# Cross attention with its context rows padded to 3072 bytes, its operands at one remainder of 512, and its shared context tails loaded two chunks at a time

## The chip, the cores and the metric

The kernel runs on one core of a Trainium2 chip. The metric is the device time of one launch in microseconds (us); lower is better.

## The reference

A decoder layer on x (32 examples of 100 tokens, 512 wide) with a context of 32 x 722 x 512, everything in float32. A layer norm without learned scale follows each of its three parts. Cut to what matters:

```python
x = layernorm(x + self_attention(x))                 # 16 heads of 32, with a distance factor
x = layernorm(x + cross_attention(x, context))       # the part that changes
x = layernorm(x + ffn(x))                            # 512 -> 1536 (gate, up) -> 512

def cross_attention(x, c):                           # per example: x 100 x 512, c 722 x 512
    q, k, v = x @ Wq.T + bq, c @ Wk.T + bk, c @ Wv.T + bv
    scores = q * 32**-0.5 @ k.T                      # per head, 100 x 722
    return softmax(scores) @ v @ Wo.T + bo
```

## The kernel before

Three stages follow each other. Tiles whose names begin with A_ and C_ belong to self attention and its output and query projections, D_ to cross attention, E_ to the output projection of cross attention and the feed-forward part. Each float32 operand of a projection is split into a high part (rounded to the matmul's format) and a low part (the rest), and a product takes three matmuls: high x high, high x low and low x high. With 512 inputs in four chunks of 128, `products` (L68) issues 12 matmuls into one bank of PSUM. Each matmul has a weight load of its own (a stationary operand of 128 columns, 512 bytes in each partition), which the profile shows as PEld beside the matmul before it.

**Cross attention** runs over 32 examples b, 8 steps for each. For each example TensorE makes 8 *key units* (4 groups of four heads, called quads, times two halves of the context: stationary a slice of `cross_wk`, moving 362 or 360 columns of the context, `HALVES`) and up to 6 *value units* (stationary 128 rows of the context, moving 512 columns of `cross_wv`). For each quad it makes the scores (`scores`, in even steps) and, six steps after a quad's first step, the weighted sum (`weighted_sum`, 48 matmuls). All units take turns in two banks, `D_ps_p`; a unit waits (`wait_bank`) until the bank that was filled two units before has been read. So that reading is ordered, too: ScalarE reads the values of a step (`take_values`) behind `normalise_second` of that step, which waits for the reciprocal that VectorE makes behind its transposes.

Between scores and weighted sum lie: VectorE's maxima, ScalarE's exponentials, the reciprocal, the normalising (GpSimd the first head of a step, ScalarE the second), VectorE's transposes of 32 x 32 blocks into `D_turned` (`turn_blocks`), and 16 DMAs for each quad that move the blocks to other partitions, `D_turned` to `D_pT`: 12 from SP's queue (`move`, L1361), 4 from ScalarE's. `D_turned` has two buffers, so `turn_blocks` of quad n waits until the moves of quad n - 2 have landed.

**SP's queue** is strictly in program order. For each b: the queries of b + 1 (`load_q`), the moves of quad 4b - 1, two chunks of the context of b + 2 (`load_ctx`), the moves of quad 4b, the store of b - 1, the moves of 4b + 1, two more chunks of the context, the moves of 4b + 2.

**Tails.** 722 context rows are five tiles of 128 and a rest of 82. To save value units, the rests of four examples share three tiles of 128 rows (examples 4q + 2 to 4q + 5, for q = 0 to 6). `load_tails(q)` loads them raw into `D_tails_raw`, all four chunks, with six DMAs, in iteration b = 4q - 1 (for q = 0 before the loop). GpSimd splits them chunk by chunk (`split_tails`, high L1496, low L1499), at the steps 8(4q + 1) + (-2, 1, 2, 3, 6, 6, 9, 9) of `TAIL_STEP`: high of chunk 0, low of chunk 0, high of chunk 1, and so on. Only then are the raw tiles free.

**Places in SBUF.** Each tile begins at a multiple of 32 bytes. The weights `cross_wk`, `cross_wv` (8192 bytes for each part) and `D_ctx0` (even examples) begin at one remainder of 512, that of `nc.sbuf_base`. A chunk of the context takes 722 x 4 = 2888 bytes = 5 x 512 + 328, a part 11552 = 22 x 512 + 288, and both parts of an example `one_ctx` = 23104 = 45 x 512 + 64. So the chunks of the two examples' buffers lie at many remainders. `E_wo` begins at `raw_at`, the activations `E_acts` at `even_at` = `nc.sbuf_base`; between the two lie 2 x 23104 = 90 x 512 + 128 bytes. The hidden tiles of the feed-forward part (30720 = 60 x 512 bytes each, token tiles of 512 bytes) and its weight pieces 5 to 11 (6144 = 12 x 512) both begin a multiple of 512 from `rest_at`.

Of the kernel before, what the change touches and what calls it, by code (L numbers as in the profile page):

```python
# [8 lines left out]
B, T, S, D, H = 32, 100, 722, 512, 16  # L9
HD = D // H  # L10
# [113 lines left out]
def phase_self_attention(nc, sem, passed, xT, wq, wk, wv, w, v, v_d, rows_d, o_d, x, bo, bq, x1_d, cq_d, raws, cross_w,  # L124
# [25 lines left out]
    with ExitStack() as ctx, ExitStack() as of_attention, ExitStack() as of_units, ExitStack() as of_outputs:  # L150
# [117 lines left out]
        for s in range(B):  # L268
# [25 lines left out]
        ctx0 = Split(lambda n, shape, dt: nc.alloc_sbuf_tensor_at(n, shape, dt, offset=ctx_at + (n[-3:] == "low") * 4 * KD * S),  # L294
                     "D_ctx0", [P, KD, S])
# [21 lines left out]
        with nc.Block() as block:  # L317
# [182 lines left out]
            def _(pool):  # L500
# [79 lines left out]
                for g in range(NG):  # L580
                    for i in range(TT):
                        n = TT * g + i
                        pool.wait_ge(eps_done, n + 1)
                        wait(pool, x1_done, n - 1)
                        pool.tensor_tensor(rstd[n % 2][:, :], var_eps[n % 2][:, :], minus_half[:, :], ALU.pow)\
                            .then_inc(rstd_done, 1)
                        if i + 2 < TT:
                            add_bias(g, i + 2)
                        elif g < 2:
                            add_bias(g + 1, i + 2 - TT)  # L590
                    if 2 <= g < NG - 1:
                        add_bias(g + 1, 0)
                        add_bias(g + 1, 1)
                    if 1 <= g < NG - 1:
                        for i in range(TT):
                            low_o(g + 1, i)
                    if 1 <= g < 3:
                        c_low(pool, [g + 1])
                for k in range(KD):
                    pool.wait_ge(ctx0_high, k + 1)  # L600
                    pool.tensor_tensor(ctx0[1][:, k, :], ctx0_raw[k], ctx0[0][:, k, :].bitcast(F32), ALU.subtract)\
                        .then_inc(ctx0_low, 1)
# [3 lines left out]
            def _(act):  # L606
# [116 lines left out]
                for k in range(KD):  # L723
                    act.activation(ctx0[0][:, k, :], ctx0_raw[k], ACT.Copy).then_inc(ctx0_high, 1)
# [311 lines left out]
def phase_cross_and_feed_forward(nc, sem, passed, ctxT, cq_d, held, bk, bv, o_d, x1_d, wo, bo, w_gate, w_up, w_down, biggest, out):  # L1036
# [20 lines left out]
    HALVES = ((0, 362), (362, S))  # L1057
# [25 lines left out]
    with ExitStack() as ctx:  # L1083
        W, ident, minus_half, biggest1, biggest_all, inexact, ctx0, q_stored = held
        every_weight = 2 * 2 * KD * D * 4
        one_ctx = 2 * KD * S * 4
# [51 lines left out]
        first_x1 = [*x1b, None, None, middle("E_x1_last", [P, D])]  # L1138
        r = {"a": middle("E_r_a", [P, D])}
        y = [middle(f"E_y{i}", [P, D]) for i in range(2)]  # L1140
        first_x1[2:4] = y
        stats = {n: even("E_stats_" + n, [P, 6]) for n in "ab"}
        mv = {n: even("E_mv_" + n, [P, 2]) for n in "ab"}
        var_eps = {n: even("E_var_eps_" + n, [P, 1]) for n in "ab"}
        rstd = {n: even("E_rstd_" + n, [P, 1]) for n in "ab"}
# [5 lines left out]
        x2 = first("E_x2", [P, TT, D])  # L1151
        r["b"] = odd("E_r_b", [P, D])
# [29 lines left out]
        t_loaded, t_high, t_low = sem("D_t_loaded"), sem("D_t_high"), sem("D_t_low")  # L1182
# [93 lines left out]
        x1_loaded, x1b_done = [sem("E_x1_loaded0"), sem("E_x1_loaded1")], sem("E_x1b_done")  # L1276
        y_done, t_done, th_done, tl_done = (sem("E_" + n) for n in ("y_done", "t_done", "th_done", "tl_done"))
# [39 lines left out]
        def x1_rows(g, i):  # L1317

            return (x1b[i % 2] if later(g) else first_x1[i])[:, :]
# [5 lines left out]
        with nc.Block() as block:  # L1325

            @block.sync
            def _(sp):
# [8 lines left out]
                def load_tails(q):  # L1337
                    wait(sp, t_low, KD * q)
                    for i in range(3):
                        sp.dma_start(tails_raw[:, :, i * P:i * P + LAST], c_rows[4 * q + 2 + i, :, :, FULL:S])\  # L1340
                          .then_inc(t_loaded, 16)
                    for i in range(3):
                        first, end = FULL + THIRD * i, min(FULL + THIRD * (i + 1), S)
                        sp.dma_start(tails_raw[:, :, (i + 1) * P - THIRD:(i + 1) * P - THIRD + end - first],
                                     c_rows[4 * q + 5, :, :, first:end]).then_inc(t_loaded, 16)
# [86 lines left out]
                for i in range(TT):  # L1432
                    sp.dma_start(first_x1[i][:, :], x1_d[col(i * P, P), :]).then_inc(x1_loaded[i % 2], 16)
# [3 lines left out]
                sp.wait_ge(u_done, len(unit_count))  # L1437
                load_weights(0)
# [30 lines left out]
            def _(pool):  # L1469
# [12 lines left out]
                def split_piece(b, k):  # L1482
                    if k == 0:
                        wait(pool, u_done, max((unit_count[i] for i in unit_count if i[1] == b - 2), default=0))
                    wait_apart(pool, c_loaded[k % 2], 32 * (b - 1) + 16 * (k // 2) + 16, passed)
                    pool.tensor_copy(cs[b % 2][0][:, k, :], craw[k % 2][:, :]).then_inc(c_high, 1)
                    pool.wait_ge(c_high, KD * b + k + 1)
                    pool.tensor_tensor(cs[b % 2][1][:, k, :], craw[k % 2][:, :],  # L1488
                                       cs[b % 2][0][:, k, :].bitcast(F32), ALU.subtract).then_inc(c_low, 1)

                def split_tails(q, k, low):
                    if k == 0 and not low:
                        wait(pool, u_done, unit_count["v", 4 * q, ST - 1] if q else 0)
                        pool.wait_ge(t_loaded, 96 * (q + 1))
                    if not low:
                        pool.tensor_copy(tails[0][:, k, :], tails_raw[:, k, :]).then_inc(t_high, 1)  # L1496
                    else:
                        pool.wait_ge(t_high, KD * q + k + 1)
                        pool.tensor_tensor(tails[1][:, k, :], tails_raw[:, k, :], tails[0][:, k, :].bitcast(F32),  # L1499
# [4 lines left out]
                def add_bias(g, i):  # L1504
                    if later(g):
                        pool.wait_ge(x1_loaded[i % 2], 16 * slot_count(g, i) + 16)
                    else:
                        pool.wait_ge(x1_loaded[i % 2], 16 * slot_count(1, i % 2))
# [631 lines left out]
```

## Time and profile before

| | |
|---|---|
| median of 3 runs | 2404.95 us (2403.91 to 2406.62) |
| profiled execution: its own time | 2403.91 us |
| profiled execution: span in the trace | 2402.1 us, mean granted TensorE clock 0.992 |
| TensorE busy | 2351.1 us of the span (98%) |
| VectorE, GpSimd, ScalarE busy | 1510.7, 1384.9, 1330.2 us |

The span goes from the first to the last instruction. Matmuls are pipelined and their ends are modelled, so the time that one takes from the stream is the distance between the starts of two neighbours, not its busy time. A granted clock of 1.00 is 2.4 GHz, 0.50 is 1.2 GHz. SP is not among the busy engines: its rows give the time that it spends issuing DMAs.

### The profile page before, as it was taken

The page shows a single profiled execution, that of the slowest core. Times are in us where ns is not written, and L with a number is a line of the kernel's source. Part 1 is how long each engine was busy: PE and PEld are TensorE (multiplying, and loading weights), DVE is VectorE, ACT ScalarE, POOL GpSimd, SP SyncE. Part 2 cuts the span into 40 slices and gives each one's busy share as a digit, 9 for nine tenths or more (in the row PEclk, how much of TensorE's full clock was granted, in tenths as well). Part 3 has the DMA queues.
Part 4 walks back from the last instruction along what each step waited for, and adds up shares of the span by engine and source line. Part 5 has one row for each costly group of instructions (what it writes and reads, how often), then busy time and mean ns, then how long its engine had stood idle before and what let it go on. Part 6 is the DMA issues. An engine that isn't in the chain of part 4 may idle for free.

```text
span 2402.1 us, 58639 instructions
## 1 busy us (share of the span) xinstructions
PE 2351.1 (98%) x21642; PEld 2041.4 (85%) x21642; DVE 1510.7 (63%) x2562; ACT 1330.2 (55%) x3322; POOL 1384.9 (58%) x1212
## 2 busy tenths in 40 slices
PE   8999989999999999999999999999999899999999
PEld 7888758988888888888888888888888699998998
DVE  4666688836767677676767677676766734435342
ACT  5888852236666666666666666666666541221321
POOL 4777577447667567566666667667664533333332
PEclk9999989999999999999999999999999999999999
DMA  7444468537677777777776776777677831102010
GB/s 193 133 127 123 119 192 323 203 105 198 185 194 200 192 199 190 193 203 197 183 206 190 201 195 190 197 196 196 186 193 201 240 124 43 49 17 65 5 35 23
DMA packets 254121, 384.59 MB, mean 160 GB/s; under 512 B 116056, under 2 KB 131480, under 8 KB 253848
## 3 DMA queue, kind: packets, MB, share of 16 engines
q1 hardware_dynamic: 229272, 330.65, 48.5%
q10 hardware_dynamic: 24576, 50.36, 8.3%
q8 instruction: 164, 2.69, 0.5%
q14 instruction: 109, 0.89, 0.1%
HBM read 126.33 MB, written 40.60 MB: 69 GB/s over the span
## 4 chain that ended last, share of the span: by engine, by line
PE 75%; DVE 1%; issue 1%; SPq 1%; DMA 1%; POOL 1%; ACT 0%; ACTq 0%; DVEq 0%; POOLq 0%
PE D_ps_p L68 42%; PE D_ps_s L1941 7%; PE D_ps_p L1968 6%; PE E_ps_g L68 6%; PE E_ps_u L68 6%; PE E_ps_d L68 5%; PE E_ps_y L68 3%; SPq L1361 1%; DVE D_columns L1745 0%; PE E_ps_t L1994 0%; ACT D_e L1610 0%; DVE D_turned L1759 0%; DMA D_pT<-D_turned 0%; DMA E_w_int<-in_w_gate 0%; POOL E_acts_low L1533 0%
## 5 line engine op out<-in xcount | busy, mean ns | idle before, releaser
L1473 POOL TENSOR_SCALAR D_e<-D_e,D_columns 128x722 f32<-128x722 f32 x256 | 538.5, 2104 | 468.2 <-DVE D_columns L1751 468.1
L1610 ACT ACTIVATE D_e<-D_ps_s,D_columns 128x723 f32<-128x723 f32 x512 | 437.7, 861 | 392.5 <-DVE D_columns L1745 347.6
L1745 DVE TENSOR_REDUCE D_columns<-D_ps_s 128x1 f32<-128x723 f32 x512 | 439.6, 900 | 296.6 <-PE D_ps_s L1941 296.5
L1759 DVE STREAM_TRANSPOSE D_turned<-D_e 128x768 f32<-128x768 f32 x512 | 496.2, 973 | 14.0 <-DMA D_pT<-D_turned 13.2
L68 PE MATMUL D_ps_p<-D_ctx_high,cross_wk_high 128*128 128x362 f32 (+1 forms) x1024 | 350.1, 342 | 1.9 <-DVEq L1771 1.5
L68 PE MATMUL D_ps_p<-D_ctx_low,cross_wk_high 128*128 128x362 f32 (+1 forms) x1024 | 336.7, 329 | 0.0
L68 PE MATMUL D_ps_p<-D_ctx_high,cross_wk_low 128*128 128x362 f32 (+1 forms) x1024 | 334.9, 327 | 0.0
L68 PE MATMUL D_ps_p<-cross_wv_high,D_ctx_high 128*128 128x512 f32 (+1 forms) x656 | 259.7, 396 | 0.0
L68 PE MATMUL D_ps_p<-cross_wv_high,D_ctx_low 128*128 128x512 f32 (+1 forms) x656 | 259.3, 395 | 0.0
L68 PE MATMUL D_ps_p<-cross_wv_low,D_ctx_high 128*128 128x512 f32 (+1 forms) x656 | 257.7, 393 | 0.0
L1617 ACT ACTIVATE D_e<-D_e,D_columns 128x722 f32<-128x722 f32 x256 | 231.0, 902 | 8.9 <-DVE D_columns L1751 8.9
L68 PEld LDWEIGHTS D_ps_p<-D_ctx_high,cross_wk_high 128*128 128x128 f32 x1024 | 192.5, 188 | 24.5 <-issue 19.4
L1528 POOL TENSOR_TENSOR E_hidden_low<-E_gated,E_hidden_high 128x320 fp32r<-128x320 f32 x120 | 104.9, 876 | 186.0 <-ACT E_hidden_high L1675 186.0
L1488 POOL TENSOR_TENSOR D_ctx_low<-D_craw,D_ctx_high 128x722 fp32r<-128x722 f32 x124 | 198.7, 1603 | 17.7 <-issue 7.1
L646 ACT ACTIVATE A_e<-A_e,A_neg_max 100x100 f32<-100x100 f32 x512 | 186.1, 367 | 40.9 <-DVE A_neg_max L773 40.6
L68 PEld LDWEIGHTS D_ps_p<-D_ctx_low,cross_wk_high 128*128 128x128 f32 x1024 | 193.2, 189 | 2.4
L1941 PE MATMUL D_ps_s<-D_keys,D_queries 32*128 32x241 f32 (+1 forms) x3072 | 192.5, 378 | 2.6 <-ACT D_e L1610 2.6
L68 PEld LDWEIGHTS D_ps_p<-D_ctx_high,cross_wk_low 128*128 128x128 f32 x1024 | 193.0, 188 | 0.0
L1852 DVE SCALAR_TENSOR_TENSOR E_gated<-E_ps_u,E_gated 128x320 f32<-128x320 f32 x120 | 59.0, 492 | 212.5 <-ACT E_gated L1682 212.5
L1941 PEld LDWEIGHTS D_ps_s<-D_keys,D_queries 32*128 32x128 f32 x3072 | 134.1, 184 | 59.9 <-issue 49.5
L1599 ACT ACTIVATE D_values<-D_ps_p 128x512 f32<-128x512 f32 (+1 forms) x185 | 110.0, 595 | 96.1 <-PE D_ps_p L68 96.0
L1968 PEld LDWEIGHTS D_ps_p<-D_pT,D_values 128*32 128x32 f32 x5920 | 126.0, 108 | 39.6 <-issue 38.9
(257 smaller groups left out, 5248.5 us busy)
## 6 DMA issues: line engine op xcount, KB each, us to landing
D_pT<-D_turned SPq DMA_DIRECT2D x1536, 96.0 KB, 2.5
D_pT<-D_turned ACTq DMA_DIRECT2D x512, 96.0 KB, 2.7
D_craw<-in_ctxT SPq DMA_DIRECT2D x124, 361.0 KB, 4.0
self_v<-wstage SPq DMA_DIRECT2D x25, 256.0 KB, 2.5
A_v<-self_v SPq DMA_DIRECT2D x32, 200.0 KB
self_o<-A_o SPq DMA_DIRECT2D x32, 200.0 KB, 3.6
x<-C_x SPq DMA_DIRECT2D x5, 1280.0 KB, 5.2
cross_q<-C_qo SPq DMA_DIRECT2D x20, 320.0 KB, 4.0
```

Source lines behind the costliest of these rows:

```text
L68: last = pe.matmul(out, lhs(a, k), rhs(b, k), start=(k == 0 and n == 0), stop=(k == chunks - 1 and n == len(terms) - 1))
L646: act.activation(head, head, ACT.Exp, bias=neg_max[:, b % 2, h:h + 1], accum_out=rowsum[:, half, i:i + 1]).then_inc(exp_done, 1)
L1473: pool.tensor_scalar(head, head, inv[:, 2 * (s % 2):2 * (s % 2) + 1], None, ALU.mult)\
L1488: pool.tensor_tensor(cs[b % 2][1][:, k, :], craw[k % 2][:, :], cs[b % 2][0][:, k, :].bitcast(F32), ALU.subtract).then_inc(c_low, 1)
L1528: pool.tensor_tensor(hs[1][:, c, cols], gated[u % 2][:, :], hs[0][:, c, cols].bitcast(F32), ALU.subtract).then_inc(hl_done, 1)
L1599: act.activation(vs[b % 2][0:rows, i, :], bank("v", b, i)[0:rows, 0:D], ACT.Copy).then_inc(v_done, 1)
L1610: act.activation(e[n // 2 % 2][:, n % 2, 0:PARTS * PART].rearrange("p (a c) -> p a c", a=PARTS), parts_of(n), ACT.Exp, bias=neg_max[:, n % ...
L1617: act.activation(head, head, ACT.Copy, scale=inv[:, 2 * (s % 2) + 1:2 * (s % 2) + 2])\
L1745: dve.tensor_reduce(neg_max[:, n % 4:n % 4 + 1], parts_of(n), AX.XY, ALU.max, negate=True)\
L1759: dve.transpose(turned[quad % 2][:, :, 2 * (s % 2) + h, :].rearrange("p j (t r) -> p t j r", r=32), e[s % 2][:, h, :].rearrange("p (t j r) ...
L1941: return pe.matmul(of_head[:, j, a, 0:end - first], qs[rows, m, :, :].rearrange("p a q -> p (a q)"), ks[rows, m, first:end], start=True, s ...
L1968: last = pe.matmul(out[HD * j:HD * (j + 1), 0:T], values[:, c:c + HD], pT[quad % 2][:, :, j, 32 * i:32 * i + QB], start=(i == 0), stop=(i ...
```

## The change

- A context chunk is spaced 768 x 4 = 3072 bytes (`ROW`) in `D_ctx0` and `D_ctx1`; only its first 722 columns are written and read. The halves of the keys become 384 and 338 columns. `one_ctx` becomes 24576 = 48 x 512.
- `D_tails` and `D_values_fourth` are placed right behind `D_ctx1`, so that all of them, the weights and the context chunks begin at one remainder of 512. `E_wo` begins there too, since `raw_at - even_at` is now 96 x 512.
- The room comes from `D_tails_raw`: two chunks in place of four. `load_tails(q, k)` loads one chunk with six DMAs and waits until the low part of the chunk that had its half before is done (`t_low` at 4q + k - 1). Chunks 0 and 1 are loaded where all four were loaded before; chunk 2 at the end of iteration b = 4q, behind the moves of quad 16q + 2; chunk 3 in iteration b = 4q + 1, behind the moves of quad 16q + 4.
- Small tiles of the E stage change places; the last tile of `x1` is loaded later, into `E_x2`, behind the last unit. GpSimd's split of the first context waits for `biggest_done`, since its place now reaches a tile that is read for it.

```diff
+ROW = 768
...
+                pool.wait_ge(biggest_done, 3 * KD)
                 for k in range(KD):
                     pool.wait_ge(ctx0_high, k + 1)
...
-    HALVES = ((0, 362), (362, S))
+    HALVES = ((0, ROW // 2), (ROW // 2, S))
...
-        one_ctx = 2 * KD * S * 4
+        one_ctx = 2 * KD * ROW * 4
...
-        cs = [ctx0, Split(inputs, "D_ctx1", [P, KD, S])]
+        cs = [ctx0, Split(inputs, "D_ctx1", [P, KD, ROW])]
         raw_at = inputs.at
-        craw = [inputs(f"D_craw{i}", [P, S]) for i in range(2)]
-
-        tails_raw = inputs("D_tails_raw", [P, KD, 3 * P])
         tails = Split(inputs, "D_tails", [P, KD, 3 * P])
         fourth = [inputs(f"D_values_fourth{i}", [P, D]) for i in range(2)]
+        craw = [inputs(f"D_craw{i}", [P, S]) for i in range(2)]
+        tails_raw = inputs("D_tails_raw", [P, 2, 3 * P])
...
-                def load_tails(q):
-                    wait(sp, t_low, KD * q)
+                def load_tails(q, k):
+                    n = KD * q + k
+                    wait(sp, t_low, n - 1)
                     for i in range(3):
-                        sp.dma_start(tails_raw[:, :, i * P:i * P + LAST], c_rows[4 * q + 2 + i, :, :, FULL:S])\
-                          .then_inc(t_loaded, 16)
+                        sp.dma_start(tails_raw[:, k % 2, i * P:i * P + LAST], c_rows[4 * q + 2 + i, :, k, FULL:S])\
+                          .then_inc(t_loaded[k % 2], 16)
...
-                load_tails(0)
+                load_tails(0, 0)
+                load_tails(0, 1)
                 for b in range(B - 1):
                     load_q(b + 1)
...
                     move(QUADS * b)
+                    if b % 4 == 1 and b // 4 < FOURS:
+                        load_tails(b // 4, 3)
                     if b > 0:
                         store(b - 1)
...
                     if b % 4 == 3 and (b + 1) // 4 < FOURS:
-                        load_tails((b + 1) // 4)
+                        load_tails((b + 1) // 4, 0)
+                        load_tails((b + 1) // 4, 1)
                     move(QUADS * b + 1)
...
                     move(QUADS * b + 2)
+                    if b % 4 == 0 and b // 4 < FOURS:
+                        load_tails(b // 4, 2)
...
+                load_first_x1(TT - 1)
                 load_weights(0)
...
                     if not low:
-                        pool.tensor_copy(tails[0][:, k, :], tails_raw[:, k, :]).then_inc(t_high, 1)
+                        pool.wait_ge(t_loaded[k % 2], 96 * (2 * q + k // 2 + 1))
+                        pool.tensor_copy(tails[0][:, k, :], tails_raw[:, k % 2, :]).then_inc(t_high, 1)
```

## Rows read from the trace of the kernel before

**Rows 1.** The page: span, and busy us with share of each engine.
```profile
span 2402.1 us, 58639 instructions
PE 2351.1 (98%) x21642; PEld 2041.4 (85%) x21642; DVE 1510.7 (63%) x2562; ACT 1330.2 (55%) x3322; POOL 1384.9 (58%) x1212
```

**Rows 2.** Busy us by stretch: cross attention's steady part; PEclk is the clock.
```profile
520.00:1860.00 1340.00, 1339.45 (x13957) 1141.74 (x13956) 927.23 (x1612) 866.00 (x1691) 870.98 (x671) 1.00 0.72 194
```

**Rows 3.** Timeline of PE: first and last of 12 matmuls, key unit, value unit.
```profile
1200.42 0.33 PE L68 MATMUL D_ps_p<-D_ctx_high,cross_wk_high 128*128 128x360 f32 x1
...
1202.25 0.32 PE L68 MATMUL D_ps_p<-D_ctx_high,cross_wk_low 128*128 128x360 f32 x1
1202.41 0.39 PE L68 MATMUL D_ps_p<-cross_wv_high,D_ctx_high 128*128 128x512 f32 x1
...
1204.97 0.39 PE L68 MATMUL D_ps_p<-cross_wv_high,D_ctx_low 128*128 128x512 f32 x1
```

**Rows 4.** Timeline of PE, E stage: within 24 E_ps_d matmuls, then 12 E_ps_y.
```profile
2004.15 0.39 PE L68 MATMUL E_ps_d<-E_w_f32r,E_hidden_low 128*128 128x512 f32 x1
...
2006.67 0.39 PE L68 MATMUL E_ps_d<-E_w_f32r,E_hidden_high 128*128 128x512 f32 x1
...
2009.16 0.40 PE L68 MATMUL E_ps_d<-E_w_f32r,E_hidden_low 128*128 128x512 f32 x1
2009.39 0.40 PE L68 MATMUL E_ps_y<-E_wo_high,E_acts_high 128*128 128x512 f32 x1
...
2011.95 0.40 PE L68 MATMUL E_ps_y<-E_wo_high,E_acts_low 128*128 128x512 f32 x1
```

**Rows 5.** Groups of PE by shape: count | busy us, mean ns | idle before.
```profile
L68 PE MATMUL D_ps_p<-cross_wv_high,D_ctx_high 128*128 128x512 f32 x640 | 253.4, 396 | 0.0
...
L68 PE MATMUL D_ps_p<-D_ctx_low,cross_wk_high 128*128 128x362 f32 x512 | 169.0, 330 | 0.0
...
L68 PE MATMUL D_ps_p<-cross_wv_high,D_tails_high 128*128 128x512 f32 x84 | 33.1, 395 | 0.0
```

**Rows 6.** Timeline of GpSimd and SP's queue near 740 us: start, length.
```profile
724.03 8.73 SPq L1361 DMA_DIRECT2D D_pT<-D_turned  x12
732.81 0.59 SPq L1349 DMA_DIRECT2D D_qraw<-cross_q  x1
733.50 7.54 SPq L1361 DMA_DIRECT2D D_pT<-D_turned  x12
...
740.32 0.99 POOL L1499 TENSOR_TENSOR D_tails_low<-D_tails_raw,D_tails_high 128x384 fp32r<-128x384 f32 x1
```

**Rows 7.** Timeline of SP's queue: the six loads of four tail chunks.
```profile
1014.52 1.65 SPq L1340 DMA_DIRECT2D D_tails_raw<-in_ctxT  x3
1016.22 1.87 SPq L1344 DMA_DIRECT2D D_tails_raw<-in_ctxT  x3
```

**Rows 8.** The moves in the stretch from 520 us: time from issue to landing.
```profile
DMA to landing us min/median/max: 2.0/2.6/9.5
```

**Rows 9.** Timeline of PE: weighted sum of quad 19 and the key unit behind.
```profile
751.33 1.24 PE L1968 MATMUL D_ps_p<-D_pT,D_values 128*32 128x100 f32 x48
752.49 0.43 PE L68 MATMUL D_ps_p<-D_ctx_high,cross_wk_high 128*128 128x362 f32 x1
```

**Rows 10.** Timelines of VectorE and ScalarE: a first transpose of quad 21, values.
```profile
747.28 0.97 DVE L1759 STREAM_TRANSPOSE D_turned<-D_e 128x768 f32<-128x768 f32 x1
...
750.33 0.59 ACT L1599 ACTIVATE D_values<-D_ps_p 128x512 f32<-128x512 f32 x1
```

**Rows 11.** Busy us by stretch at the end of cross attention, columns as in 2.
```profile
1870.00:1877.50 7.50, 3.86 (x77) 2.59 (x75) 5.95 (x12) 5.41 (x11) 7.50 (x6) 1.00 1.03 288
1877.50:1881.00 3.50, 3.47 (x8) 2.79 (x9) 2.44 (x4) 2.45 (x6) 3.50 (x3) 0.51 1.09 284
```

**Rows 12.** VectorE's maxima of the integer weights; GpSimd's first work in cross attention.
```profile
L844 DVE TENSOR_TENSOR biggest<-biggest,C_piece_max x9: 159/627/1076, 406.6 to 479.1; 128x1 f32<-128x1 f32 x9
...
492.22 1.38 POOL L1543 MEMSET D_tails_raw<- 128x1536 f32 x1 [8.92 <-POOLq L317]
```

More of the change, by code:

```diff
@@ L293, in phase_self_attention @@
         ctx_at = nc.sbuf_base
-        ctx0 = Split(lambda n, shape, dt: nc.alloc_sbuf_tensor_at(n, shape, dt, offset=ctx_at + (n[-3:] == "low") * 4 * KD * S),
-                     "D_ctx0", [P, KD, S])
+        ctx0 = Split(lambda n, shape, dt: nc.alloc_sbuf_tensor_at(n, shape, dt, offset=ctx_at + (n[-3:] == "low") * 4 * KD * ROW),
+                     "D_ctx0", [P, KD, ROW])
         ctx0_raw = [staging[k // 2][:, :, :].rearrange("p k n -> p (k n)")[:, k % 2 * S:(k % 2 + 1) * S] for k in range(KD)]
@@ L723, in _ @@
                 for k in range(KD):
-                    act.activation(ctx0[0][:, k, :], ctx0_raw[k], ACT.Copy).then_inc(ctx0_high, 1)
+                    act.activation(ctx0[0][:, k, 0:S], ctx0_raw[k], ACT.Copy).then_inc(ctx0_high, 1)
                 act.wait_ge(ctx0_high, KD)
@@ L1137, in phase_cross_and_feed_forward @@
         x1b = [middle(f"E_x1b{i}", [P, D]) for i in range(2)]
-        first_x1 = [*x1b, None, None, middle("E_x1_last", [P, D])]
-        r = {"a": middle("E_r_a", [P, D])}
+        r = {"a": even("E_r_a", [P, D])}
         y = [middle(f"E_y{i}", [P, D]) for i in range(2)]
[L1141 to L1145, printed above, removed]
+        stats = {n: middle("E_stats_" + n, [P, 6]) for n in "ab"}
+        mv = {n: middle("E_mv_" + n, [P, 2]) for n in "ab"}
+        var_eps = {n: middle("E_var_eps_" + n, [P, 1]) for n in "ab"}
+        rstd = {n: middle("E_rstd_" + n, [P, 1]) for n in "ab"}
         EARLY = 5
@@ L1151, in phase_cross_and_feed_forward @@
         x2 = first("E_x2", [P, TT, D])
+        first_x1 = [t[:, :] for t in (*x1b, *y)] + [x2[:, TT - 1, :]]
         r["b"] = odd("E_r_b", [P, D])
@@ L1317, in x1_rows @@
         def x1_rows(g, i):
-            return (x1b[i % 2] if later(g) else first_x1[i])[:, :]
+            return x1b[i % 2][:, :] if later(g) else first_x1[i]
         def place(t, n):
@@ L1335, in load_ctx @@
                     sp.dma_start(craw[k % 2][:, :], c_rows[b, :, k, :]).then_inc(c_loaded[k % 2], 16)
[L1337 to L1338 removed]
+                def load_tails(q, k):
+                    n = KD * q + k
+                    wait(sp, t_low, n - 1)
                     for i in range(3):
[L1340 to L1341 removed]
+                        sp.dma_start(tails_raw[:, k % 2, i * P:i * P + LAST], c_rows[4 * q + 2 + i, :, k, FULL:S])\
+                          .then_inc(t_loaded[k % 2], 16)
                     for i in range(3):
                         first, end = FULL + THIRD * i, min(FULL + THIRD * (i + 1), S)
[L1344 to L1345 removed]
+                        sp.dma_start(tails_raw[:, k % 2, (i + 1) * P - THIRD:(i + 1) * P - THIRD + end - first],
+                                     c_rows[4 * q + 5, :, k, first:end]).then_inc(t_loaded[k % 2], 16)
                 def load_q(b):
@@ L1431, in _, with load_first_x1 @@
                 sp.dma_start(bo_b[:, :], bo.rearrange("(a n) -> a n", a=1).broadcast_to([P, D])).then_inc(bo_loaded, 16)
-                for i in range(TT):
-                    sp.dma_start(first_x1[i][:, :], x1_d[col(i * P, P), :]).then_inc(x1_loaded[i % 2], 16)
+                def load_first_x1(i):
+                    sp.dma_start(first_x1[i], x1_d[col(i * P, P), :])\
+                      .then_inc(x1_loaded[i % 2] if i < TT - 1 else x1_last_loaded, 16)
+                for i in range(TT - 1):
+                    load_first_x1(i)
                 move(last - 3)
```

20 lines of the change are left out of this document (11 added, 9 removed).

## The prediction

> **What bounds the kernel now.** I read the page first: TensorE is busy 98% of the span, the others at most 63% [rows 1]. Then the busy time by stretch: in cross attention's steady part, 1340 us and more than half of the span, TensorE is busy 1339.45 us at the full clock [rows 2]. So there a nanosecond saved for each matmul is saved from the time, and every us for which TensorE has to wait is added to it. Next the timeline of TensorE, for the distance between starts. A value unit's 12 matmuls start from 1202.41 to 1204.97 us, 2.56/11 = 232.7 ns apart, a key unit's 360-column ones 1.83/11 = 166.4 ns apart [rows 3]. At 2.4 GHz 512 and 360 columns are 213.3 and 150.0 ns, so 19.4 and 16.4 ns come on top of the columns.
>
> Last SP's queue, since the change adds DMAs and waits there. The 12 moves of a quad take it 7.54 to 8.73 us, and those of the next begin 9.47 us after those of the last (724.03, 733.50) [rows 6]. It is in order and has little room. The reader is to see the lead that it has: the last of the moves of quad 19 is issued at 733.50 + 7.54 = 741.04 and lands about 2 us later, and the weighted sum of this quad starts at 751.33 [rows 6, 8, 9]: some 8 us.
>
> **Alignment, the gain.** The trace has 512-column matmuls whose two operands begin at one remainder of 512 (E_ps_d) beside others that lie 128 bytes apart (E_ps_y), at one clock. E_ps_y: 2.56/11 = 232.7 ns, as the value units. E_ps_d: (2009.16 - 2006.67)/11 = 226.4 ns once the run is settled, (2006.67 - 2004.15)/11 = 229.1 ns in the eleven before [rows 4]. So one remainder is worth 3.6 ns early in a run and 6.3 ns late. A value unit is 12 long, but its neighbours will be aligned too: I take 5.0. There are 3 x (640 + 84) = 2172 such matmuls [rows 5]: 10.9 us (7.8 to 13.7). The key matmuls, 6 x 512 = 3072 [rows 5] (the 360-column groups have the same count), have 16.4 ns over their columns, and the aligned run 13.0 at the best, 15.8 early: 0.6 to 3.4 ns, middle 2.0: 6.1 us (1.8 to 10.4). 384 + 338 columns are as many as 362 + 360. `E_wo` gets the activations' remainder: 300 matmuls by 5.0 ns, 1.5 us. Together **-18.5 us** (-10.7 to -26).
>
> There is a rule against this term. The Trainium skill, "TensorE: Matmul & The Clock Gate", Part 2, step-by-step, says that TensorE reads the moving operand and the next weights through two independent ports, so that loading weights takes nothing from the running matmul. By it the remainders of the two could not matter and this term would be 0; the two runs in [rows 4], of one shape and clock, speak against it.
>
> **The tail loads, the price.** Chunk 2 of the tails goes where chunk 0 lay, so SP may load it only after the low part of chunk 0. It is placed behind the moves of quad 16q + 2. For q = 1: these moves are issued by 724.03 + 8.73 = 732.76; the low part of chunk 0 ends at 740.32 + 0.99 = 741.31 [rows 6]. SP stands for 8.5 us, and behind it stand `load_q` and the moves of quad 19, which before began at 733.50. Step by step:
>
> - 741.31: SP goes on. Six loads take 3.57 us before [rows 7]; the new ones move a quarter of the bytes each, but issue costs by the instruction, as far as these rows go (`load_q` costs 0.59): 3.5 (1.8 to 3.6). 744.8.
> - `load_q` 0.7: 745.5. The 12 moves 7.54 to 8.73 [rows 6], I take 8.1: 753.6.
> - The last one lands 2.6 us after its issue began (2.0 at the least) [rows 8], 2.0 after it ended: 755.6.
> - The weighted sum of quad 19, at 751.33 before [rows 9], waits 4.3 us.
> - What is late next: the transposes of quad 21 use the buffer that these moves read. The first stood at 747.28 and would now be at 755.6, 8.3 us late. Behind it in order stand the reciprocals, ScalarE's normalising and the values read out at 750.33 to 750.92: 3.64 us after that transpose began [rows 10]. So 759.2. The key unit behind the weighted sum fills the bank that these values leave; it began at 752.49 [rows 9]. TensorE loses 759.2 - 752.49 = 6.7 us in all.
>
> This comes for each q from 0 to 6, as the program repeats by four examples: 7 x 6.7 = **+47 us**. Bounds: with loads at half the issue time, moves at 7.54 and landing 1.4 us behind, the transpose is at 752.7 and the loss 3.9: 27 us. With 3.6, 8.73 and 2.0 it is at 756.3 and the loss 7.5: 52 us. Nothing earlier gives it back: TensorE has no idle time to fill.
>
> **Chunks 0 and 1** are 12 loads where six stood: 3.5 us later for the moves behind, six times (q = 1 to 6). Without delay a weighted sum has 8 us in hand; six loads take 3.6 of them now, 3.5 more leave 1. The transposes behind have 752.49 - 750.92 = 1.57 us [rows 9, 10]. I take 0.5 for each: **+3 us** (0 to 12). Chunk 3 waits for work that is long done by then, and its 3.5 us fall where SP is already late and TensorE too: 0.
>
> **The clock.** After 7.5 us in which TensorE was busy for 3.86, the next 3.5 us had a granted clock of 0.51, the level of 1.2 GHz [rows 11]. The new wait, 4.3 us and 2.4 us around one weighted sum, leaves TensorE as idle. 3.4 us at half clock lose 1.7 us, of which part falls into the second wait: 0 to 1.7 each, I take 0.9, **+6 us** (0 to 12).
>
> **At nothing.** GpSimd's split of the first context may now begin only after the last maximum, at about 479.7; it ended at 492.22 - 8.92 = 483.3 and then waited 8.92 us for the stage to begin [rows 12]. A delay of 3 us or so is covered by that; without it, 3 us once. The smaller memset behind it saves under a us that nothing waits for. The copies into padded rows, and ScalarE's 384 or 338 columns in place of 362 and 360, are as many elements on engines with a third of their time free [rows 2]. The late load of the last `x1` tile costs SP one issue, 0.6 us, at the end.
>
> **Sum**, against the profiled execution's own 2403.9 us (1 us below the median shown): 2403.9 + 47 + 3 + 6 - 18.5 = **2441 us**.
>
> **Rivals and chances.**
>
> 1. As above, both mechanisms: 2441 us. 0.60.
> 2. *Alignment brings nothing*, because the difference in [rows 4] comes from something else in these runs (their length, the neighbours): 2403.9 + 47 + 3 + 6 = 2460 us. For it: the spacings of units differ little; against it: two values in one stage at one clock. 0.15. The Trainium skill's rule on two independent ports, weighed above, would bring this.
> 3. *Only half of the stall*: the weighted sum waits 4.3 us, but the chain behind it is absorbed (ScalarE's order has slack that I don't see) and the clock holds: 7 x 4.3 = 30; 2403.9 + 30 - 18.5 = 2415 us. For it: engines beside TensorE are idle a third of the time; against it: bank and order force the chain. 0.15.
> 4. *The stall is hidden, and it is faster*: the wait costs only SP's lead. It decides at the transpose: it may start 1.57 us late, at 748.85, so SP would have to go on by about 734.5 rather than 741.3. That needs the low part of chunk 0 some 7 us earlier against the moves. Then 2403.9 - 18.5 = 2385 us. For it: SP has leads of 8 us elsewhere; against it: GpSimd's place for this operation isn't moved. 0.08.
>
> 0.02 is left for more (a longer half clock). To break even, the loss would have to be 18.5/7 = 2.6 us at each of the seven places; the lower bound is 3.9.
>
> **Range.** Low: 27 us of stall, no clock, 26 us of gain: 2405. High: 52 + 12 + 6 - 11: 2463. I give 2407 to 2464, which holds the first two cases and most of the third. The three runs lie 2.7 us apart, so 0.2%, 4.8 us, is about what a measurement tells from no change. Faster: case 4, 0.08. Within 0.2%: the lower part of case 3, 0.05. Slower: 0.87.
>
> **What the profile of the changed kernel would show.** Seven places, one for every four examples, where the weighted sum of quad 16q + 3 waits for the moves (some 4 us), and the key unit behind it for ScalarE's values (some 2.4 us); in SP's queue a gap of 8 us before the loads of chunk 2, released by GpSimd's low part of chunk 0; VectorE's transposes waiting for moves far longer than before. Value matmuls 227 to 229 ns apart, 384-column keys 173 to 175 (160.0 + 13 to 15), E_ps_y 227 to 229. Half-clock stretches behind some of the seven. It would be wrong if SP were not kept waiting there, if the weighted sum found its moves landed, or if the distances stayed at 233 ns.

## The result, and the profile after

The changed kernel takes 2454.9 us (median of 6 runs, 2451.93 to 2455.83) where the one before took 2404.55 in runs beside it: 1.0207 times as long, 95% interval 1.0197 to 1.0217. That is slower by 50 us; the forecast was 2441 with a range of 2407 to 2464. All medians in this document are of fast runs; the only slow ones are two of the eleven of the kernel with late loads on the layout of before (2567 and 4147 us).

The profiled execution took 2455.3 us. The page of the changed kernel, busy time and share of each engine as in [rows 1]:

```profile
span 2453.5 us, 58766 instructions
PE 2360.7 (96%) x21642; PEld 2055.6 (84%) x21642; DVE 1509.0 (62%) x2562; ACT 1335.4 (54%) x3322; POOL 1402.4 (57%) x1212
```

The span is 51.4 us longer, and TensorE's busy time only 9.6 us. So TensorE waits, or works slowly, or both. What it waits for in the steady part of cross attention (520 to 1900 us; total us, times, longest us):

```profile
PE D_ps_p L1983 <- DMA D_pT<-D_turned: 25.5, 7, 4.2
PE D_ps_p L69 <- ACT D_values L1614: 12.0, 11, 2.2
```

L1983 is the weighted sum (L1968 before), L69 the helper of the projections (L68 before), L1614 the values read out. Seven weighted sums wait for their moves, and the units behind them for ScalarE. Together 37.5 us; in [rows 2] TensorE was idle for half a microsecond. The changed kernel's waits of SP's queue and of VectorE (the latter from 520 to 1900 us) show what lies ahead of that:

```profile
SPq L1342 <- POOL D_tails_low L1512: 65.0, 7, 11.4
...
DVE D_turned L1774 <- DMA D_pT<-D_turned: 135.9, 44, 9.2
```

One of the seven places, step by step: the changed kernel's timelines around 760 us, GpSimd, SP's queue, TensorE, VectorE, ScalarE, in this order (start, length; in brackets the idle time before and what ended it):

```profile
747.33 1.00 POOL L1512 TENSOR_TENSOR D_tails_low<-D_tails_raw,D_tails_high 128x384 fp32r<-128x384 f32 x1
...
748.36 2.58 SPq L1342 DMA_DIRECT2D D_tails_raw<-in_ctxT  x3
750.98 1.39 SPq L1346 DMA_DIRECT2D D_tails_raw<-in_ctxT  x3
752.41 0.43 SPq L1351 DMA_DIRECT2D D_qraw<-cross_q  x1
752.94 7.59 SPq L1363 DMA_DIRECT2D D_pT<-D_turned  x12
...
762.17 1.25 PE L1983 MATMUL D_ps_p<-D_pT,D_values 128*32 128x100 f32 x48 [3.98 <-DMA D_pT<-D_turned]
765.63 0.69 PE L69 MATMUL D_ps_p<-D_ctx_high,cross_wk_high 128*128 128x384 f32 x1 [2.21 <-ACT D_values L1614]
766.12 0.52 PE L69 MATMUL D_ps_p<-D_ctx_low,cross_wk_high 128*128 128x384 f32 x1
766.44 0.52 PE L69 MATMUL D_ps_p<-D_ctx_high,cross_wk_low 128*128 128x384 f32 x1
...
762.22 0.98 DVE L1774 STREAM_TRANSPOSE D_turned<-D_e 128x768 f32<-128x768 f32 x1 [7.97 <-DMA D_pT<-D_turned]
...
764.20 0.90 ACT L1632 ACTIVATE D_e<-D_e,D_columns 128x722 f32<-128x722 f32 x1 [7.68 <-DVE D_columns L1766]
765.00 0.58 ACT L1614 ACTIVATE D_values<-D_ps_p 128x512 f32<-128x512 f32 x1
```

GpSimd ends the low part at 748.33; SP goes on at 748.36, issues six loads, the queries' load and twelve moves until 760.53; the moves have landed at 762.17, when the weighted sum starts 3.98 us late. In the same moment VectorE starts its transposes, 7.97 us late; ScalarE's normalising and values follow, and the key unit behind the weighted sum has waited 2.21 us more. That is the prediction's chain, with 13.84 us from the end of the low part to the weighted sum where 14.3 (741.31 to 755.6) were forecast, 3.46 to the key unit (3.6 forecast), and 6.19 us of idle TensorE (6.7 forecast).

The last two TensorE rows start 0.32 us apart for 384 columns. That is the lower clock. The changed kernel's windows at the seven places (TensorE busy, then the granted clock):

```profile
582.48:589.28 6.80, 5.34 (x56) 0.50 0.76 230
763.38:770.18 6.80, 4.59 (x18) 0.50 0.71 210
940.87:951.11 10.24, 8.06 (x67) 0.50 0.84 227
1121.78:1132.02 10.24, 8.14 (x67) 0.50 0.77 216
1302.70:1309.50 6.80, 5.11 (x57) 0.50 0.87 261
1483.58:1490.38 6.80, 4.83 (x30) 0.50 0.89 247
1661.10:1671.30 10.20, 7.35 (x64) 0.50 0.81 226
sum 57.88, PE 43.43; mean PE 6.20
```

At each of the seven the clock is granted at 0.50, 1.2 GHz, for 6.8 or 10.2 us. That begins in the first wait, in the weighted sum behind it or in the second wait; the two waits of a place are 3.9 to 6.2 us together. In [rows 2] its mean was 1.00. TensorE works for 43.43 us of these. At 2.4 GHz the same key matmuls start 0.173 us apart (the rows below), so 1 - 0.173/0.320 = 46% of that is lost: an estimate of 20 us.

The other side, the gain. The changed kernel's timeline of TensorE, the second and the last of twelve 384-column matmuls, first and last of twelve 338-column ones, of a value unit and, in the last stage, of an `E_ps_y` run:

```profile
750.09 0.34 PE L69 MATMUL D_ps_p<-D_ctx_low,cross_wk_high 128*128 128x384 f32 x1
...
751.82 0.33 PE L69 MATMUL D_ps_p<-D_ctx_high,cross_wk_low 128*128 128x384 f32 x1
752.00 0.31 PE L69 MATMUL D_ps_p<-D_ctx_high,cross_wk_high 128*128 128x338 f32 x1
...
753.68 0.31 PE L69 MATMUL D_ps_p<-D_ctx_high,cross_wk_low 128*128 128x338 f32 x1
753.84 0.39 PE L69 MATMUL D_ps_p<-cross_wv_high,D_ctx_high 128*128 128x512 f32 x1
...
756.37 0.39 PE L69 MATMUL D_ps_p<-cross_wv_high,D_ctx_low 128*128 128x512 f32 x1
...
2053.34 0.39 PE L69 MATMUL E_ps_y<-E_wo_high,E_acts_high 128*128 128x512 f32 x1
...
2055.84 0.39 PE L69 MATMUL E_ps_y<-E_wo_high,E_acts_low 128*128 128x512 f32 x1
```

384 columns: 1.73/10 = 173.0 ns, 13.0 over the columns. 338: 1.68/11 = 152.7, 11.9 over. Values: 2.53/11 = 230.0 where [rows 3] had 232.7. `E_ps_y`: 2.50/11 = 227.3 where [rows 4] had 232.7. Single units vary, so here are the means over all of cross attention, worked out from the starts in each trace: distance from a matmul to the next, less columns/2.4 GHz, those left out that are over 60 ns more than that or end at other work (up to 13 in 100 of a kind).

```
ns over the columns       keys, 1st half  keys, 2nd half  values  tails  E_ps_y
before                    16.6 (362)      15.1 (360)      19.0    19.2   19.8
changed                   14.7 (384)      13.6 (338)      16.8    16.8   14.7
changed, in pairs         14.7 (384)      13.5 (338)      16.8    16.8   14.6
changed, late, 128 off    15.9 (384)      18.0 (338)      19.4    19.9   19.9
```

(The last two rows are kernels of the next section.) From the first to the second: keys 3072 x 1.7 ns = 5.2 us, values and tails 3 x (656 + 84) = 2220 x 2.2 = 4.9 (48 more than the prediction counted), `E_ps_y` 300 x 5.1 = 1.5. Together 11.6 us, where 18.5 were forecast.

The place in a unit tells more, from the same starts: of a unit's twelve value matmuls (185 units), the changed kernel's first nine are at 17.7 ns over the columns and the last three at 13.3. Before, both groups are at 19.0 to 19.1.

The balance of the changed kernel: waits 37.5, clock 20, alignment -11.6, and the stage begins 1.7 us later (its first key unit at 494.0, before at 492.3): 47.6 of 51.4 us. 3.8 us are not placed. The later start need not be the change's: among the kernels below with the same work ahead of the stage it begins at 491.1 to 495.0.

### The profile page after: what moved, and what is told of

It is laid out like the page before. It is cut to its first block, busy times and chain, and to the rows that moved or that the text cites. A ratio compares the mean times of both kernels' runs of the same rounds, so it can differ in the third digit from the quotient of the medians.

```text
span 2453.5 us, 58766 instructions
## 1 busy us (share of the span) xinstructions
PE 2360.7 (96%) x21642; PEld 2055.6 (84%) x21642; DVE 1509.0 (62%) x2562; ACT 1335.4 (54%) x3322; POOL 1402.4 (57%) x1212
## 3 DMA queue, kind: packets, MB, share of 16 engines
q10 hardware_dynamic: 24576, 50.36, 7.9%
## 4 chain that ended last, share of the span: by engine, by line
PE 59%; SPq 8%; issue 4%; POOL 3%; DVE 2%; DMA 2%; ACTq 1%; ACT 1%; DVEq 0%; POOLq 0%
PE D_ps_p L69 31%; PE E_ps_g L69 6%; PE E_ps_u L69 6%; SPq L1363 5%; PE D_ps_s L1956 5%; PE E_ps_d L69 5%; PE D_ps_p L1983 4%; PE E_ps_y L69 3%; POOL D_e L1486 2%; DMA D_pT<-D_turned 1%; SPq L1342 1%; DVE D_turned L1774 1%; SPq L1346 1%; ACTq L1641 1%; DVE D_columns L1760 1%
## 5 line engine op out<-in xcount | busy, mean ns | idle before, releaser
L1774 DVE STREAM_TRANSPOSE D_turned<-D_e 128x768 f32<-128x768 f32 x512 | 495.0, 972 | 143.3 <-DMA D_pT<-D_turned 141.2
L69 PE MATMUL D_ps_p<-D_ctx_high,cross_wk_high 128*128 128x384 f32 (+1 forms) x1024 | 353.0, 345 | 14.9 <-ACT D_values L1614 12.8
L69 PE MATMUL D_ps_p<-D_ctx_low,cross_wk_high 128*128 128x384 f32 (+1 forms) x1024 | 340.0, 332 | 0.0
L69 PE MATMUL D_ps_p<-D_ctx_high,cross_wk_low 128*128 128x384 f32 (+1 forms) x1024 | 339.4, 331 | 0.0
L69 PE MATMUL D_ps_p<-cross_wv_low,D_ctx_high 128*128 128x512 f32 (+1 forms) x656 | 258.0, 393 | 0.0
L69 PE MATMUL D_ps_p<-cross_wv_high,D_ctx_low 128*128 128x512 f32 (+1 forms) x656 | 257.5, 393 | 0.0
L69 PE MATMUL D_ps_p<-cross_wv_high,D_ctx_high 128*128 128x512 f32 (+1 forms) x656 | 256.1, 390 | 0.0
L69 PEld LDWEIGHTS D_ps_p<-D_ctx_high,cross_wk_high 128*128 128x128 f32 x1024 | 197.1, 193 | 38.9 <-issue 18.9
L1501 POOL TENSOR_TENSOR D_ctx_low<-D_craw,D_ctx_high 128x722 fp32r<-128x722 f32 x124 | 216.8, 1748 | 17.7 <-issue 7.1
L69 PEld LDWEIGHTS D_ps_p<-D_ctx_low,cross_wk_high 128*128 128x128 f32 x1024 | 197.7, 193 | 2.2
L69 PEld LDWEIGHTS D_ps_p<-D_ctx_high,cross_wk_low 128*128 128x128 f32 x1024 | 197.4, 193 | 0.0
L1983 PEld LDWEIGHTS D_ps_p<-D_pT,D_values 128*32 128x32 f32 x5920 | 130.3, 110 | 65.0 <-issue 36.9
L1983 PE MATMUL D_ps_p<-D_pT,D_values 128*32 128x100 f32 x5920 | 159.6, 255 | 25.8 <-DMA D_pT<-D_turned 25.5
```

What stands on the lines that cost most here:

```text
L69: last = pe.matmul(out, lhs(a, k), rhs(b, k), start=(k == 0 and n == 0), stop=(k == chunks - 1 and n == len(terms) - 1))
L1501: pool.tensor_tensor(cs[b % 2][1][:, k, 0:S], craw[k % 2][:, :], cs[b % 2][0][:, k, 0:S].bitcast(F32), ALU.subtract).then_inc(c_low, 1)
L1774: dve.transpose(turned[quad % 2][:, :, 2 * (s % 2) + h, :].rearrange("p j (t r) -> p t j r", r=32), e[s % 2][:, h, :].rearrange("p (t j r) ...
L1983: last = pe.matmul(out[HD * j:HD * (j + 1), 0:T], values[:, c:c + HD], pT[quad % 2][:, :, j, 32 * i:32 * i + QB], start=(i == 0), stop=(i ...
```

## Experiments

**The wait alone.** Theory: SP's wait for the low part of chunk 0 makes the loss, through the clock too. The kernel before, with that wait and no loads behind it:

```diff
                     move(QUADS * b + 2)
+                    if b % 4 == 0 and b // 4 < FOURS:
+                        sp.wait_ge(t_low, KD * (b // 4) + 1)
```

> The kernel before with one thing added: SP's queue waits for the low part of tail chunk 0 behind the moves of quad 16q+2, seven times, and loads nothing there. Theory (the wait makes the loss): by the rows of before the moves of quad 19 then land at 752.1, the key unit behind is 3.3 us late, 7 x 3.3 = 23 us, and some of the clock: 2430 us (2422 to 2440). Rival (the loads make it): 2404 to 2410 us.

2430.89 us, ratio 1.0101 (1.0086 to 1.0117): 24 us lost by a wait that loads nothing. The waits in its trace from 520 to 1900 us:

```profile
PE D_ps_p L68 <- ACT D_values L1601: 16.0, 10, 2.2
PE D_ps_p L1970 <- DMA D_pT<-D_turned: 3.2, 4, 0.9
```

Without the six loads (some 4 us) the weighted sum hardly waits, but the second wait, of the values behind the transposes, is all there, and the clock is lower for a while at five of the seven places, 17 us in all. So the wait alone costs about half, and the loads behind it the rest.

**The tail loads without the alignment.** The layout of before, with the changed kernel's `load_tails(q, k)` and its four places:

```diff
-        tails_raw = inputs("D_tails_raw", [P, KD, 3 * P])
+        tails_raw = inputs("D_tails_raw", [P, 2, 3 * P])
...
-                load_tails(0)
+                load_tails(0, 0)
+                load_tails(0, 1)
```

> The kernel before, its places and row spacing untouched, with the tail loads of the change alone: two raw chunks, one chunk for each set of six loads, issued and waited for where the change has them. Theory (all of the loss comes from these loads and their wait, the places give a gain of 8 to 12 us): 2465 us (2458 to 2475), TensorE waiting some 25 us for D_pT in seven places. Rival (the new places do the harm): within 10 us of the kernel before.

2459.67 us, ratio 1.0224 (1.0209 to 1.0240). The whole loss and a little more is here, and in the trace the same seven places:

```profile
PE D_ps_p L1975 <- DMA D_pT<-D_turned: 25.0, 7, 4.2
PE D_ps_p L68 <- ACT D_values L1606: 12.7, 10, 2.2
```

It lies only 0.0017 (4 us) above the changed kernel, not 11 or 12. Part of that is the clock: here it was low for 6.8 us at each place, 48 us in all, in the changed kernel for 58.

**What the clock costs.** The changed kernel with 18 matmuls ahead of each of the seven weighted sums, into the bank that this sum then overwrites (their results are thrown away):

```diff
+                    if quad % 16 == 3 and quad // 16 < FOURS:
+                        wait_bank(pe, "o", quad, 0)
+                        for i in range(18):
+                            pe.matmul(bank("o", quad, 0)[:, 0:D], W[0][0][:, i % KD, 0:P], W[1][0][:, i % KD, :],
+                                      start=True, stop=True)
                     pe.wait_ge(moved_sem(quad), moved_count(quad))
```

> The changed kernel with 18 extra matmuls of 512 columns (some 4.1 us, their results are thrown away) before each of the seven weighted sums that wait: TensorE works through the wait in place of standing idle. Theory (half of what the change lost beyond its waits is the half clock that follows them): granted clock 1.00 nearly throughout cross attention, 2437 us (2430 to 2445). Rival (the clock costs as little as I forecast, 6 us): 2448 us or more.

2448.63 us, ratio 1.0177 (1.0156 to 1.0198), the rival's time, but not for the rival's reason. The theory's number was too low because work had been added, too: the 18 take 4.30 us (755.33 to 759.63 in its timeline), 30 us at seven places, where only 24 us of the first wait went away, and units behind wait longer for their values.

```profile
PE D_ps_p L69 <- ACT D_values L1614: 16.8, 18, 2.2
PE D_ps_p L1988 <- DMA D_pT<-D_turned: 1.4, 2, 1.1
```

So TensorE has 30.1 - 24.1 + 4.8 = 10.8 us more to do or to wait for, and cross attention, from its first key unit to its last matmul, still is 6.0 us shorter (1480.2 us in this trace, 1486.1 in the changed kernel's). The clock gave back 17 us, with 6.8 us of low clock still left. To see it with the waits filled in full, the same with 22:

```diff
-                        for i in range(18):
+                        for i in range(22):
```

> The changed kernel with 22 matmuls of 512 columns (results thrown away) ahead of each of the seven weighted sums that wait, in place of 18: at the 0.239 us that each took, 7 x 22 x 0.239 = 36.8 us, as much as TensorE waits at these places in the changed kernel in all (25.5 + 12.0 us). So the waits are replaced by work of the same length, and what the time falls by is the clock alone. Theory: 18 us, as the kernel with 18 gives when its added work and waits are set off: 2437 us, granted clock 1.00 throughout. Rival: the 6 us of the prediction, 2449 us. A second rival: about 23 us, what was left over in the balance of the changed kernel: 2432 us.

2441.49 us, ratio 1.0165 (1.0146 to 1.0183). Its windows and waits from 520 us:

```profile
520.00:1860.00 1340.00, 1328.23 (x13735) 1131.18 (x13734) 898.12 (x1566) 846.69 (x1642) 872.88 (x658) 1.00 0.70 188
```

```profile
PE D_ps_p L69 <- ACT D_values L1614: 11.0, 19, 1.2
```

The filling at the place around 760 us in its timeline:

```profile
754.01 5.28 PE L1977 MATMUL D_ps_p<-cross_wv_high,cross_wk_high 128*128 128x512 f32 x22
759.23 1.25 PE L1988 MATMUL D_ps_p<-D_pT,D_values 128*32 128x100 f32 x48
```

The clock's mean is 1.00, and no weighted sum waits. 7 x 5.22 = 36.5 us of filling (754.01 to 759.23) and 11.0 us of waits stand where 37.5 us of waits stood, 10 us more. The median is 13.4 us less than the changed kernel's, the ratio 0.0042 (10 us) less, and cross attention in the trace 11.9 us shorter (1474.2). So the clock was worth 20 to 23 us; by the rows of half clock it is 20, by the kernel with 18 matmuls 17 or more. That lies between the theory's 18 and the upper rival's 23, and the runs don't part the two. The time itself is above both their forecasts, since 10 us of waits were left. The forecast of 6 is out.

**The alignment without the wait.** Chunk 2 loaded where the changed kernel loads chunk 3, and chunk 3 one set of moves behind that, so that neither waits for work that is still to be done:

```diff
                     move(QUADS * b)
                     if b % 4 == 1 and b // 4 < FOURS:
-                        load_tails(b // 4, 3)
+                        load_tails(b // 4, 2)
...
+                    if b % 4 == 1 and b // 4 < FOURS:
+                        load_tails(b // 4, 3)
                     move(QUADS * b + 2)
-                    if b % 4 == 0 and b // 4 < FOURS:
-                        load_tails(b // 4, 2)
```

> The changed kernel, with the loads of chunks 2 and 3 of the tails issued later: chunk 2 behind the moves of quad 16q+4, chunk 3 ahead of the moves of quad 16q+6, when the low parts that they wait for are long done. Theory (the loss is SP standing at the wait for the low part of chunk 0): SP's queue has no wait of over 1 us for D_tails_low, TensorE waits in cross attention for D_pT under 2 us in all instead of 25.5, no half clock between 520 and 1860 us; only the alignment is left, about 12 us by the distances measured in the changed kernel: 2393 us (2386 to 2400). Rival (the loss comes from 24 loads in place of 6, whatever they wait for): still 2430 us or more, with SP's transposes and moves late.

2405.26 us, ratio 1.000 (0.9991 to 1.0009): the loss is gone, the gain isn't there, and the theory's 2393 is missed. And the same edit on the layout of before, with `D_tails_raw` of two chunks:

> The kernel before, places and row spacing untouched, with two raw chunks of tails and the late loads of the first run of this call. Theory: as the kernel before, 2404 us (2401 to 2409), so that the difference to the first run is the alignment alone, some 12 us. Rival (alignment is worth nothing, and the distances differ for another reason): the two runs take the same time.

2410.29 us (median of nine runs), ratio 1.0023 (1.0013 to 1.0032). The aligned one is 5.0 us faster, fewer than the 12 expected. (A later expectation has 7.7 us for this difference: it counts from 2412.97, the median of all eleven runs.) Both still have a stall, and the faster TensorE waits more in it. From 520 to 1880 us it waits for ScalarE's values, in the aligned kernel and in the other:

```profile
PE D_ps_p L69 <- ACT D_values L1614: 11.7, 15, 2.3
...
PE D_ps_p L68 <- ACT D_values L1606: 9.1, 10, 1.8
```

For ScalarE's exponentials it waits 3.0 and 0.9 us. 5.0 + 2.6 + 2.1 = 9.7 us. The stall that is left shows in VectorE's transposes, which wait for moves, in the aligned kernel and in the kernel before (520 to 1900 us):

```profile
DVE D_turned L1774 <- DMA D_pT<-D_turned: 88.6, 36, 5.3
...
DVE D_turned L1759 <- DMA D_pT<-D_turned: 13.2, 7, 4.5
```

SP waits for GpSimd's low part for 1.1 us in all, so that wait isn't the cause. What is left as a cause is the number of loads in SP's queue; the next two experiments try that.

**Loads less bunched.** As the aligned kernel with late loads, with chunk 1 loaded behind the moves of quad 16q - 2 (16q + 14 of the group before) and not straight behind chunk 0:

```diff
                         load_tails((b + 1) // 4, 0)
-                        load_tails((b + 1) // 4, 1)
...
                     move(QUADS * b + 2)
+                    if b % 4 == 3 and (b + 1) // 4 < FOURS:
+                        load_tails((b + 1) // 4, 1)
```

> As the run before, and chunk 1 of the next tails behind the moves of quad 16q+14, so that no place has more than six loads. Theory: VectorE waits less for the moves of quads 16q+13 and 16q+14, time 0 to 4 us below the run before: 2390 us (2385 to 2398). Rival (the 12 loads in one place are hidden): no difference.

2400.91 us, ratio 0.9982 (0.9973 to 0.9991), 4.4 us below the kernel it is made from (the two intervals just touch). Its TensorE waits 8.5 us for values (before: 0.3), VectorE 62.4 us for moves.

**Fewer loads.** Two chunks in each load: 0 and 1 where the kernel before loads all four, 2 and 3 where the changed one loads chunk 3. 12 loads for four examples in place of 24, as many bytes. (In the changed kernel there is room for two chunks, but each load carries one; here it carries two.)

```diff
-                def load_tails(q, k):
-                    n = KD * q + k
-                    wait(sp, t_low, n - 1)
+                def load_tails(q, p):
+                    wait(sp, t_low, KD * q + 2 * p)
+                    chunks = slice(2 * p, 2 * p + 2)
                     for i in range(3):
-                        sp.dma_start(tails_raw[:, k % 2, i * P:i * P + LAST], c_rows[4 * q + 2 + i, :, k, FULL:S])\
-                          .then_inc(t_loaded[k % 2], 16)
+                        sp.dma_start(tails_raw[:, :, i * P:i * P + LAST], c_rows[4 * q + 2 + i, :, chunks, FULL:S])\
+                          .then_inc(t_loaded, 16)
```

> The changed kernel with chunks 0 and 1 in one set of six loads and chunks 2 and 3 in another, the second issued behind the moves of quad 16q+4: 12 loads for four examples in place of 24, and no wait that SP reaches early. Theory (what was left in the runs with late loads is the number of loads on SP's queue): TensorE waits for D_values and D_pT under 5 us in all, and the gain of the places is left: 2395 us (2389 to 2400). Rival (any stop for tails between these moves costs as much): 2400 us or more.

2394.23 us, ratio 0.9947 (0.9933 to 0.9960): faster than both kernels. Its steady part and VectorE's wait (520 to 1900 us):

```profile
520.00:1860.00 1340.00, 1338.12 (x14055) 1142.77 (x14054) 935.41 (x1626) 875.75 (x1707) 894.16 (x673) 1.00 0.73 195
```

```profile
DVE D_turned L1770 <- DMA D_pT<-D_turned: 30.4, 15, 5.3
```

TensorE is idle for 1.9 us of 1340 again, at the full clock, and has made 98 matmul records more in it than in [rows 2]. Two chunks in a load cost SP little more than one: a set of six takes it 3.68 us from first to last (mean of 14 sets), with one chunk each in the changed kernel 3.23 (mean of 28). Then the same loads on the layout of before:

> The layout of before, with the tail loads in pairs of chunks: it differs from the kernel in pairs on the new layout (0.9947 of before) by the alignment alone, and no stall of TensorE lies over either. Theory: alignment is worth the 11.7 us that the distances of matmuls summed to, and the pairs cost next to nothing, so this kernel is at the time of before, 2404 to 2408 us, and slower than the pairs on the new layout by 10 to 13 us. Rival: alignment is worth only the 7.7 us by which the two kernels with late loads differed; then this one is at 2401 to 2403 us, faster than before, and the pairs themselves save 2 to 4 us.

2405.19 us, ratio 1.0004 (0.9995 to 1.0012). Pairs cost nothing, and the alignment is the whole gain of 11.0 us (0.0057 between the ratios, 13.7 us), as the theory had it. In the two traces cross attention takes 1426.7 against 1436.0 us and what follows it 473.4 against 474.9: 10.9 us.

**One remainder, or only a spacing by 512?** The aligned kernel with late loads, with the contexts and all behind them (tails, `E_wo`) 128 bytes higher than the weights' and activations' remainder:

```diff
-        ctx_at = nc.sbuf_base
+        ctx_at = nc.sbuf_base + 128
...
-        inputs.at = odd_at
+        inputs.at = odd_at + 128
```

> The first run of this call with the context, the tails and E_wo all placed 128 bytes higher: each chunk of the context still begins a multiple of 512 from the next, but at another remainder than the weights. Theory (the two operands must begin at one remainder): value matmuls back at 232 ns, E_ps_y too, time 8 to 12 us above the first run: 2403 us. Rival (chunks spaced by a multiple of 512 are enough): within 2 us of the first run.

2417.86 us, ratio 1.0049 (1.0037 to 1.0062), 12.6 us above the same without the shift. All distances are back at those of before or wider, but for the keys' first half (the table's last row). So the rows' spacing of 3072 bytes alone gives nothing; with the common remainder it does. A rival has no run of its own: that a place 128 bytes higher is slow by itself, whatever the other operand. `E_ps_d` speaks against it: both its operands lie 128 bytes above that remainder, and it is at 14.9 ns over the columns in the kernel before, like `E_ps_y` at one remainder (14.7).

## Why the prediction was right, and where its sizes were off

**The mechanism** is the one forecast as case 1: SP held by GpSimd's low part, the weighted sum late by the moves, the key unit late by the values behind the transposes, seven times. The kernel with the wait alone and the one with the tail loads alone show that this is the cause, and the ones with late or paired loads that without it the loss goes. That the sum came as near as 14 us is in part luck: 14 us too little for the clock and 12.5 too much for the wait nearly cancel each other.

**The wait** was forecast as 7 x 6.7 = 47 us, and 3 for chunks 0 and 1; it came to 36.1 at the seven places and 1.4 at four others, 37.5 in all. At the place around 760 us it was 6.19. At the first place the weighted sum waited only 2.42 us; at four of the others the key unit waited 1.23 or 1.24 in place of 2.21, because the weighted sum ahead of it, at the lower clock, took 2.23 us and not 1.25. So a part of the forecast wait went over into the clock's term.

**The clock** is the term that was mis-sized: 0.9 us for each place, 6 in all, with 12 as the upper bound; it cost some 20 (17 to 23). It was taken from a single stretch of 3.5 us at half clock [rows 11]. Here the low clock lasted two or three times as long, TensorE was at work in three quarters of it, and each us of that work lost 46%.

**The alignment** was forecast as 18.5 us with 10.7 as the lower bound; the distances sum to 11.6, the two kernels in pairs differ by 11.0. The step that failed is the value matmuls' 5.0 ns: they gained 2.2. It was taken between the early and the settled part of the long run of [rows 4], on the ground that a unit's neighbours would be aligned too. They are, but each unit starts anew: its first nine matmuls gain 1.4 ns, the last three 5.7. The keys' 2.0 ns (1.7 measured) and the 5.0 ns of `E_ps_y` (5.1) held. The run of [rows 4] was the right neighbour for `E_ps_y`, in the same stage, and not for the value units. What in the addresses sets the distance isn't settled: 138 value matmuls of the kernel before had their moving operand at the remainder of the weights loaded beside them, by the tiles' places, and their mean was 19.3 ns, no better than the rest. The pairs do differ: sorted by how far apart the two remainders lie, the value matmuls of the kernel before run from 13.5 ns (200 bytes, 82 of them) to 22.0 (40 bytes, 164). But each pair stands at the same places of a unit, so that pair and place can't be told apart. That one remainder is the best choice isn't shown; that it is better than the mix of before and than 128 bytes apart is.

Set off against each other: 7 us less of gain, 14 more of clock, 12.5 less of wait, 1.7 of a later start and the 3.8 that are not placed make the 14 us between the forecast and the result.

**Rival 2**, no gain from alignment, is refuted by the kernels in pairs. For it the prediction had drawn on the Trainium skill, "TensorE: Matmul & The Clock Gate", Part 2, step-by-step: TensorE has two independent read ports in SBUF, one for the moving operand and one for the weights. From that it concluded that the place of the operands would change nothing; but 128 bytes of it cost 12.6 us here, and the measurement decides. Whether it is the ports that get in each other's way no run shows. **Rival 3**, only the first wait: the changed kernel waits 12.0 us for the values, too, and the clock falls at all seven places; with the wait alone it is even 16.0 us for the values and 3.2 for the moves. **Rival 4**, hidden: it would have needed the loads elsewhere; put there, in pairs, they give 2394 and not 2385, as the gain is 11 us and not 18.5.

**At nothing**: GpSimd's later split of the first context stayed covered; it waited 16.1 us for the last maximum and still 6.6 us at the start of the stage.

## What to carry to other kernels

On an in-order queue with little room, count instructions ahead of bytes: taking the early wait out brought the change from +2.1% to 0.0%, and half as many loads of twice the size from there to -0.5%. A wait on such a queue is paid at every consumer behind it, and where it leaves a busy TensorE idle for some us, the clock behind it is paid as well; here it cost about half of what the wait cost. Price a gain from a neighbour in the same stage, and make it apart from the buffer that pays for it, since the two can hide each other, as the late loads did at exactly 1.000.

## What the runs showed of the hardware that was not expected

Six loads of a quarter of the bytes took SP 3.23 us from first to last (mean of the changed kernel's 28 sets), those of all four chunks 3.58 (mean of the seven sets of the kernel before). The granted clock stayed at 1.2 GHz for 6.8 or 10.2 us at each place although TensorE was at work for most of that, at one of them 5.9 us beyond the end of the last wait (1126.11 to 1132.02). A shift of the context, the tails and `E_wo` by 128 bytes widened the distance of the 338-column matmuls from 13.5 to 18.0 ns over their columns and cost 12.6 us, about what the common remainder gains. A unit of twelve value matmuls at one remainder comes down to 13.3 ns over the columns in its last three alone.
